# Edge counts of a graph kernel: sums in PSUM run on through all edges, totals are copied once per tile, and GpSimd subtracts

## The reference, cut to what matters

```python
def _sage_layer(x, src, dst, Wl, bl, Wr, num_nodes):
    msg = x[src]
    ssum = jax.ops.segment_sum(msg, dst, num_segments=num_nodes)
    deg = jax.ops.segment_sum(jnp.ones((src.shape[0], 1), x.dtype), dst, num_segments=num_nodes)
    agg = ssum / jnp.maximum(deg, 1.0)
    return agg @ Wl + bl + x @ Wr
...
src_h = h[src] @ W_msg.T + b_msg
emb = edge_embed[jnp.clip(edge_type, 0, NUM_EDGE_TYPES)]
messages = jax.ops.segment_sum(src_h + emb, dst, num_segments=num_nodes)
```

## Time and profile before

| | us |
|---|---|
| three runs | 9355.59, 9361.79, 9379.95; median 9361.79 |
| profiled execution | 9320.16 |
| its span, first to last instruction | 9318.2 |
| the adjacency stage in it, first to last matmul | 127.6 to 1644.8 |
| mean granted clock of TensorE, whole span | 0.862 |
| busy in the whole span: TensorE, VectorE, ScalarE, GpSimd | 7645.8, 5974.4, 3792.3, 5148.8 |

### The profile page before, as it was taken

The page is one execution under the profiler, slowest core; times in us unless marked ns, Lnnn a source line. Parts: engine busy times, 40 slices in busy tenths (PEclk is TensorE's granted clock), DMA queues, the critical chain, the costliest instruction groups (busy, mean ns, idle before and its releaser), DMA issues. The chain is left out here.

```text
span 9318.2 us, 197548 instructions
## 1 busy us (share of the span) xinstructions
PE 7645.8 (82%) x49731; PEld 5556.8 (60%) x49914; DVE 5974.4 (64%) x15460; ACT 3792.3 (41%) x10443; POOL 5148.8 (55%) x5386
## 2 busy tenths in 40 slices
PE   4999999988666666666666689999899999899997
PEld 1443344887444434444444467888688788688886
DVE  6999999022333333333333368888878788778888
ACT  2222222301111111111111156777666677667776
POOL 0000000000777767776777758878577787577774
PEclk9999999999677776777677779999889899899998
DMA  1000011854222222222222212222122222122221
GB/s 43 7 21 26 30 42 42 342 217 165 59 60 60 61 55 60 60 60 56 59 60 60 61 49 59 59 56 58 48 57 58 55 58 57 47 59 57 56 57 42
DMA packets 372820, 615.17 MB, mean 66 GB/s; under 512 B 114410, under 2 KB 277569, under 8 KB 355988
## 3 DMA queue, kind: packets, MB, share of 16 engines
q0 software_dynamic: 150528, 308.58, 12.7%
q1 hardware_dynamic: 221460, 296.64, 9.2%
HBM read 509.70 MB, written 94.96 MB: 65 GB/s over the span
## 5 line engine op out<-in xcount | busy, mean ns | idle before, releaser
L535 POOL DMA_INDIRECT rows_and_onehots<-node_table,idx x4704 | 4978.7, 1058 | 1367.8 <-issue 1185.3
L762 PEld LDWEIGHTS ps<-rows_and_onehots,w 128*128 128x128 f32 x5280 | 1029.2, 282 | 1717.7 <-issue 1675.8
L762 PE MATMUL ps<-rows_and_onehots,w 128*128 128x128 f32 x5280 | 1098.6, 376 | 1085.8 <-issue 1050.3
L530 POOL COPY idx<-src_g 128x8 int32 (+1 forms) x594 | 152.5, 257 | 2642.3 <-DMA node_table<-hr 2549.3
L1219 DVE TENSOR_TENSOR w<-rows_and_onehots,ps 128x512 f32<-128x512 f32 x663 | 456.2, 688 | 1726.9 <-POOLq L546 1361.8
L656 ACT ACTIVATE w<-w 128x512 f32<-128x512 f32 x663 | 417.3, 629 | 2589.0 <-DVE w L1219 2589.0
L859 PE MATMUL ps<-w_L_conv_edge,ea 65*128 65x512 f32 x1326 | 974.1, 828 | 31.7 <-DMA ea<-in_ea 26.1
L712 ACT ACTIVATE hr<-iota_d,dloc 128x128 f32<-128x128 f32 x2724 | 871.0, 390 | 2.1 <-issue 1.3
L908 PE MATMUL ps<-w_L_gnn_We,hr 128*128 128x512 f32 x1344 | 824.7, 698 | 33.8 <-issue 30.0
L912 PEld LDWEIGHTS ps<-xrb,hr 128*128 128x128 bf16 x8064 | 569.3, 106 | 450.2 <-issue 450.2
L613 ACT ACTIVATE xrb<-iota_d,local_dst 128x128 f32<-128x128 f32 x976 | 298.7, 389 | 1085.5 <-DVE local_dst L1133 1085.5
(11 more groups left out here) (240 smaller groups left out, 12650.0 us busy)
## 6 DMA issues: line engine op xcount, KB each, us to landing
rows_and_onehots<-node_table,idx POOLq DMA_INDIRECT x4704
hr<-in_ea SPq DMA_DIRECT2D x672, 64.0 KB
w<-adjacency_turned SPq DMA_DIRECT2D x26, 1600.0 KB, 6.9
adjacency<-rows_and_onehots SPq DMA_DIRECT2D x25, 1600.0 KB, 5.2
w<-adjacency SPq DMA_DIRECT2D x25, 1600.0 KB, 12.0
rows_and_onehots<-adjacency_turned SPq DMA_DIRECT2D x24, 1600.0 KB, 7.1
adjacency_turned<-rows_and_onehots SPq DMA_DIRECT2D x17, 1600.0 KB, 7.8
ea<-in_ea SPq DMA_DIRECT2D x672, 32.0 KB
```

What stands on the lines that cost most here:

```text
L535: pool.indirect_dma_start(out=G[q][:, (i % CH) * D:(i % CH + 1) * D], out_offset=None, in_=table[:, :], in_offset=bass.IndirectOffsetOnAxi ...
L762: m = pe.matmul(bank(u % 2, P), rows[u][:, c * D:(c + 1) * D], OH[u][:, c * P:(c + 1) * P], start=(c == 0), stop=(c == CH - 1))
```

## The change

- The adjacency stage uses the steps of all other stages, 512 edges each, 220 of them; its own tables, and the instructions that make them, are gone. One new table, `steps_to_end`, holds the number of steps up to each tile's end.
- VectorE makes all one-hots of a step, four of the targets (128 columns each, from `local_ids`, f16 numbers, and the stored `dloc`), one of the types and four of the sources, into one of two sets of buffers, and announces them once (`edge_onehots`). It waits until TensorE has finished the step before last.
- TensorE takes one pass over the banks per step, four chunks in each. `start` is set at the very first chunk only: the sums run on to the end of all edges. Before each bank it waits until the totals of the tile before have been copied out of it (`bank_copied`), for which it loads the step's tile number into a register.
- ScalarE makes no one-hots. At each tile's end it copies the eight banks to one of two rows of totals, once the store out of the row it overwrites is through (`counts_out`).
- GpSimd zeroes one row at the start and subtracts, for each tile, the last totals from the new ones, in the place of the last ones; SyncE stores that.

```diff
-            def target_onehots(s, u):
-                act.wait_ge(local_targets, s + 1)
-                ...
-            by_twos(act, target_onehots)
+            act.sem_inc(bank_copied, PARTS)
+            for t in range(TILES):
+                steps = STEPS
+                if t < TILES - 1:
+                    steps = act.value_load(steps_to_end[t:t + 1, 0:1], min_val=1, max_val=STEPS)
+                held(act, counts_out, FLUSH * t)
+                for b in range(PARTS):
+                    cs = columns_of(b) if b < BANKS else slice(NP, COUNTED)
+                    counted = ps[:, cs] if b < BANKS else bank(BANKS, TYPES + 1)
+                    act.wait_ge(bank_counted, steps * PARTS + (b + 1))
+                    act.copy(totals[t % 2][:, cs], counted).then_inc(bank_copied, 1)
...
+            begin(pool, "adjacency")
+            link(pool.memset(totals[1], 0.0))
+            for t in range(TILES):
+                old, new = totals[(t + 1) % 2], totals[t % 2]
+                pool.wait_ge(bank_copied, PARTS * (t + 2))
+                pool.tensor_tensor(old, new, old, ALU.subtract).then_inc(tile_counted, 1)
...
             def count_edges(s, u):
-                ...
+                t = pe.value_load(tile_i[0:1, bass.ds(s, 1)], min_val=0, max_val=TILES - 1)
+                pe.wait_ge(edge_onehots, s + 1)
+                for b in range(PARTS):
+                    pe.wait_ge(bank_copied, t * PARTS + (b + 1))
+                    for c in range(CH):
+                        to = ps[:, columns_of(b)] if b < BANKS else bank(BANKS, TYPES + 1)
+                        of = SOH[u % 2][c][:, columns_of(b)] if b < BANKS else TOHB[u % 2][:, c, :]
+                        m = pe.matmul(to, TARGETS[u % 2][:, c * P:(c + 1) * P], of,
+                                      start=(isinstance(s, int) and s == 0 and c == 0), stop=(c == CH - 1),
+                                      skip_group_check=True)
+                    m.then_inc(bank_counted, 1)
+
+            pe.sem_inc(bank_counted, PARTS)
+            walk(pe, count_edges, rounds=2)
...
-            link(dve.memset(counts[1], 0.0))
-            ...
-            by_twos(dve, source_onehots)
-            add_counts(STEPS_B - 1, (STEPS_B - 1) % 2)
-            dve.wait_ge(bank_added, STEPS_B * PARTS)
+
+            def edge_onehots_of(s, u):
+                held(dve, bank_counted, s * PARTS)
+                for c in range(CH):
+                    dve.tensor_scalar(TARGETS[u % 2][:, c * P:(c + 1) * P], local_ids, dloc[:, bass.ds(s * CH + c, 1)], None,
+                                      ALU.is_equal)
+                dve.tensor_tensor(TOHB[u % 2][:, :, 0:TYPES],
+                                  fields[:, bass.ds(s * 16 + 12, CH)][:, :, None].to_broadcast([P, CH, TYPES]),
+                                  iota_t[:, None, :].to_broadcast([P, CH, TYPES]), ALU.is_equal)
+                for c in range(CH):
+                    m = dve.tensor_scalar(SOH[u % 2][c], node_ids, fields[:, bass.ds(s * 16 + c, 1)], None, ALU.is_equal)
+                m.then_inc(edge_onehots, 1)
+
+            walk(dve, edge_onehots_of, rounds=2)
+            dve.wait_ge(bank_copied, PARTS * (TILES + 1))
```

More of the change, by code:

```diff
@@ L45 @@
 HALF = NP // 2
-CB = 8
-GROUPS_B = CHUNKS // CB
-STEPS_B = GROUPS_B + TILES - 1
 COUNTED = NP + TYPES + 1
@@ L201, in build @@
         OHB = [sb(f"OHB{i}", [P, CH * P], BF16) for i in range(2)]
[L202 to L208, removed]
+        TOHB = [sb(f"TOHB{i}", [P, CH, TYPES + 1], BF16) for i in range(2)]
+        SOH = [[x[:, i * HALF:(i + 1) * HALF].bitcast(BF16) for x in (w1, w2) for i in range(2)],
+               [x[:, i * HALF:(i + 1) * HALF].bitcast(BF16) for x in (hr, ht) for i in range(2)]]
+        TARGETS = [xr[:, i * CH * P // 2:(i + 1) * CH * P // 2].bitcast(BF16) for i in range(2)]
+        local_ids = node_ids[:, HALF:HALF + P]
+        totals = [arena[:, i * COUNTED:(i + 1) * COUNTED] for i in range(2)]
         by_target = [w1[:, :], w2[:, :]]
@@ L767, in _ @@
             pe.matmul(bank(1, GROUPS, 1), ones[0:TILES - 1, 0:1], past_g[0:TILES - 1, :], start=True, stop=True)
-            pe.matmul(bank(2, STEPS_B), ones[0:TILES - 1, :], past_b[0:TILES - 1, :], start=True, stop=True)
             pe.matmul(bank(0, NSP), ones[0:TILES - 1, :], past[0:TILES - 1, :], start=True, stop=True).then_inc(turn, 1)
@@ L773, in count_edges @@
             def count_edges(s, u):
-                pe.wait_ge(target_onehot, s + 1)
-                for pair in range(0, CB, 2):
-                    pe.wait_ge(source_onehot, s * CB + (pair + 2))
-                    for b in range(PARTS):
-                        if pair == 0 and not (isinstance(s, int) and s < 1):
-                            pe.wait_ge(bank_added, s * PARTS + (b + 1 - PARTS))
-                        for c in (pair, pair + 1):
-                            to = ps[:, columns_of(b)] if b < BANKS else bank(BANKS, TYPES + 1)
-                            of = SOH[c][:, columns_of(b)] if b < BANKS else TOHB[u][:, c, :]
-                            m = pe.matmul(to, OHB8[u][:, c * P:(c + 1) * P], of, start=(c == 0), stop=(c == CB - 1))
-                        if pair == CB - 2:
-                            m.then_inc(bank_counted, 1)
-                    if pair < CB - 2:
-                        m.then_inc(source_used, 1)
-            by_twos(pe, count_edges)
+                t = pe.value_load(tile_i[0:1, bass.ds(s, 1)], min_val=0, max_val=TILES - 1)
[11 more added lines that the diff above has]
+            walk(pe, count_edges, rounds=2)
             pe.wait_ge(loaded, 16 * n_loads)
@@ L1114, in _ @@
             dve.wait_ge(stored, STORES)
-            link(dve.memset(counts[1], 0.0))
-            def add_counts(s, u):
-                if not (isinstance(s, int) and s < 1):
-                    done = dve.value_load(tile_b[0:1, bass.ds(s - 1, 1)], min_val=0, max_val=TILES - 1)
-                    dve.wait_ge(counts_out, done * FLUSH + 1)
-                for b in range(PARTS):
-                    cs = columns_of(b) if b < BANKS else slice(NP, COUNTED)
-                    counted = ps[:, cs] if b < BANKS else bank(BANKS, TYPES + 1)
-                    dve.wait_ge(bank_counted, s * PARTS + (b + 1))
-                    dve.scalar_tensor_tensor(out=counts[u][:, cs], in0=counts[1 - u][:, cs], scalar=keep[:, bass.ds(s, 1)],
-                                             in1=counted, op0=ALU.mult, op1=ALU.add).then_inc(bank_added, 1)
```

81 lines of the change are left out of this document (11 added, 70 removed).

## The result

| us | before | after |
|---|---|---|
| median | 9358.69 (4 runs, 9345.98 to 9379.95) | 9240.37 (4 runs, 9219.24 to 9256.44) |
| profiled execution, its span | 9320.16, 9318.2 | 9219.24, 9217.5 |
| first to last matmul of the counting stage | 127.6 to 1644.8: 1517.2 | 119.9 to 1504.8: 1384.8 |
| first load of the next stage | 1658.7 | 1525.5 |
| first gather of the GIN stages | 2317.6 | 2178.3 |

The ratio is 0.9878, 95% interval [0.9857, 0.9898]: 118 us faster at the medians. The prediction, 9259, is 19 above the median.

A forecast was written before the change was run, and what follows sets the result against it. VectorE was taken to bound the counting stage by 1.4 us a step. New stage 1210 + 2.6 + 154 + 48 = 1414.6, with -6.0 and +5.5: -103 us, giving 9217 profiled, 9259 us median; range 9050 to 9345.

The forecast's parts named there:

- TensorE becomes the bound at 5.50 us a step: Counting stage: 220 steps of four chunks at 1.375 us a chunk, 5.50 us a step, 1210 us in all.
- rival by TensorE's own issue: Counting steps: unhidden register load and eight waits cost 2.2 us a step, 484 in all: 9743 us; chance 0.10.
- VectorE's round 4.9, spare 0.6: Counting step: VectorE's one-hots and semaphores take 4.9 us, leaving 0.6 us before TensorE needs them.
- rival in which VectorE stays the bound: Counting steps: five small instructions at 0.3 us make VectorE's round 5.66 us, the kernel 9308 us; chance 0.16.
- The subtraction 7.0: Tile's end: GpSimd subtracts 3210 f32 columns in 7.0 us, scaled from the select's 283 ns for 128 columns.
- The whole of it falls on VectorE: Tile's end: GpSimd's subtraction blocks VectorE for its whole 7.0 us, from bounds of 0 to 7.0.
- rival without exclusion: Tile's end: GpSimd's subtraction delays no one-hot, no stalls, stage 1212.6 us, kernel 9057 us; chance 0.17.
- Stalls 154: Tile ends: TensorE stands 6.4 us at each of 24 with work behind them, 154 us in all.
- Clock 48: After the tile-end stalls: TensorE restarts at a lower clock, 2.0 us each, 24 times, 48 us.
- Stage 1414.6: Counting stage: matmul steps, cold start, stalls and clock loss together take 1414.6 us, against 1517.2 before.
- Front -6.0: Before the counting stage: fewer table instructions and no VectorE memset; TensorE begins at 121.7 instead of 127.67 us.
- End +5.5: After the last counting matmul: a 0.6 us copy and a 7.2 us subtraction delay the last store by 5.5 us.

The follow-up runs named there:

- x1: The changed kernel with GpSimd's subtraction cut to the 10 type-count columns: stage 1212.6 us, ratio to the kernel before 0.9699.
- z2: The changed kernel with subtraction deferred to the products, and 3 of 4 matmuls left out in two of six source banks: stage 1029.5 us.
- y1: The changed kernel without GpSimd's subtraction, the tile before subtracted later from 128-column products and type counts: stage 1213.8 us, ratio to before 0.9769.
- x2: The changed kernel with the subtraction in eight pieces by banks, each behind its bank's copy: stage 1312.7 us, ratio to before 0.9839.
- x3: The changed kernel with the subtraction in three pieces of 1070 columns, meant for three successive steps: stage 1357.3 us, ratio to before 0.9850.
- y3: The changed kernel with GpSimd clearing the old totals by memset instead of subtracting: stage 1261.2 us, one run.
- y4: The changed kernel with GpSimd's subtraction done twice at each tile's end: stage 1528.0 us, one run.
- x4: The changed kernel unaltered, run again on another chip: stage 1386.4 us, ratio to the kernel before 0.9824.
- z1: The kernel before, unaltered, profiled on another chip: stage 1517.0 us, first load 1656.6 us.
- z3: The changed kernel unaltered, beside the kernel before on another chip: stage 1386.1 us, ratio to before 0.9856.

## Why the prediction was right, by its steps

- **TensorE becomes the bound at 5.50 us a step**: 5.504 (x1), and no gap within a tile. The rival by TensorE's own issue is out: 0.9 us of gaps in 220 steps beside the 24 stalls. One reading of the kernel before was off without changing the sum: the 355.9 us of the earlier trace rows are 2.9 us a step and not the 1.4 that TensorE loses. They are waits of weight loads, and most of them pass while a matmul is under way: TensorE was without one for 68 us of the whole stage.
- **VectorE's round 4.9, spare 0.6**: 4.7 (z2: 4.68) and 0.81. The small one-hots are 0.165 us from start to start, near the 0.15 I took; the 0.3 I added for semaphores was too much. The rival in which VectorE stays the bound needed 5.66.
- **The subtraction 7.0**: 5.87. The size came near by luck. The ten-column subtraction of x1 takes 204 ns, so 0.2 us are fixed, and from 10 to 3210 columns it is 5.67 us, 1.77 ns each. If the select has the same fixed part, which no run shows, its 283 ns leave 0.6 ns a column and would have given some 2.2 us for 3210 (an estimate). Scaling the fixed part too was one error, taking an instruction with one input for one with two the other, and they had opposite signs.
- **The whole of it falls on VectorE, the chosen end of a range from 0 to 7.0**: right, and shown by taking it away (x1, y1), cutting it (x2, x3), shortening it (y3) and doubling it (y4). The rival without exclusion is out. The rule of the Trainium skill ("SBUF — State Buffer", "Who interferes with whom"), that whoever is first blocks the other for the whole instruction, is now seen in the direction that the trace of before did not have: 248 ns became 5914. It is shown for VectorE's one-hots with one tensor and a scalar as inputs; no run tries GpSimd's pass beside other kinds of VectorE instruction.
- **Stalls 154**: 124.1, from 5.17 instead of 6.4 each. The two terms above, -1.13 and -0.2, make -1.33 of it, and -1.23 came.
- **Clock 48**: 45 (46.9 less the start). 2.0 for each was the estimate between 0 and 2.6, and 1.9 came.
- **Stage 1414.6**: 1384.8. The 30 us are the stalls. The terms counted in this profile add up to 1381.7 (1212.6 + 124.1 + 45); x4, whose trace has all 5280 wide matmuls, counts 235 at the lower level, 3 us more.
- **Front -6.0**: -7.7; VectorE started at 115.1 and not at 117.0. The tables account for 3.5 us of the 5.1 (from VectorE's first instruction to their end it is 11.1 us before and 7.6 after, 3.15 expected). The rest are two loads that landed sooner: the targets' at the start by 0.8 us, the penalties' by 0.7; why is open. Between z1 and z3 the first matmul is 6.6 us sooner.
- **End +5.5**: +6.9. The subtraction is shorter than I took it, but I missed that TensorE's clock falls in the longer wait: it was granted 0.50 over the 25 transposes of the type counts (1516.8 to 1522.3) where it had been 1.00 before, 2.6 us more.
- **The stages behind, the same code, 0**: this step failed. In the profiled pair 32 us of the 133 won at the first load were not there at the end: the GIN stages are 27 us longer, nearly all of it the slower gathers, and the GAT stages 13, which is within their spread (at the medians 118 us arrived). It made up for the 30 us by which the stage's terms were too high, so that 9217 (the sum against the profiled execution, which took 9219) is right to 2 us by two errors of opposite sign. The forecast was good by its mechanism to 30 us and not to 2.

## What to carry to other kernels

Before an idle GpSimd is given a wide elementwise pass, look at who computes in SBUF beside it: here each microsecond of it above VectorE's 0.7 to 1.0 of spare was one of TensorE's, and 180 of the 313 us that the change would have given at the first load without it (x1 against before) went that way. Ask whether the operation can be done where the data are small: subtracting 128-column products instead of 3200-column counts cost 3 to 9 us up to the first gather. If a wide pass must stay, it may pay to cut it so that each piece falls into another round of the engine that it shuts out; see then what event starts that round. That advice is argued and not shown: x2's pieces fell into two rounds and won 74 us of the stage but nothing of the whole time, x3's timing missed, and no run has each piece in a round of its own. Read an experiment in the whole time too: of 182, 79 and 180 us won at the first load (x1, x2, y1), 169, 0 and 109 showed in the medians.

## What the hardware showed that I had not expected

- A GpSimd memset, which reads nothing, holds VectorE off as a subtraction does (2.83 us, stall 1.83).
- Stalls of TensorE of 1.83 us left the granted clock at 1.00; the clock fell behind 10 of 24 stalls of 1.98 to 2.07 us and 19 of 24 of 3.14 to 3.20, for about eight wide matmuls. Those of 5.14 cost about 9 matmuls at the lower level each, those of 10.82 about 10.
- Three subtractions of 1070 columns took 2.69, 2.08 and 2.08 us, one of 3210 columns 5.87; beside the first of them VectorE had an instruction under way when it began.
- The same gather instruction takes 944, 947 or 952 to 955 ns by the program in which it stands, and keeps its value to 3 ns from chip to chip.
